# Counting the edges' sources: one-hots of 7 and 6 bits in place of 6 and 7

## The reference, cut to what matters

```
ones = jnp.ones(src.shape[0])
out_deg = jnp.maximum(jax.ops.segment_sum(ones, src, num_segments=n), 1.0)
...
scale = jnp.sqrt(out_deg[src]) * jnp.sqrt(out_deg[dst])
msg = msg / scale[:, None]
```

## Time and profile before

| | us |
|---|---|
| median of 3 runs | 3346.48 (3343.41 to 3349.89) |
| the profiled execution | 3338.86 |
| its span, first to last instruction | 3337.2 |

### The profile page before, as it was taken

How to read it: one execution, slowest core, us unless ns; L and a number is a source line. 1 busy time by engine, 2 the same in 40 slices (tenths; PEclk the granted TensorE clock), 3 DMA queues, 4 the chain that set the end, 5 groups by cost and what they waited for, 6 DMA issues and landing times.

```text
span 3337.2 us, 51572 instructions
## 1 busy us (share of the span) xinstructions
PE 2826.4 (85%) x17241; PEld 2524.3 (76%) x17241; DVE 2173.0 (65%) x5166; ACT 1530.3 (46%) x2926; POOL 1683.0 (50%) x1627
## 2 busy tenths in 40 slices
PE   8858888788888874755799898998989989899998
PEld 8837677678677764744688787887878878788887
DVE  5635555455555565645777878778787877877754
ACT  5102233233233332432456565665656656556565
POOL 0067777777777720245755555454554545543000
PEclk9988899899899986866689999999999999999999
DMA  3176666666666620576777767677676767766534
GB/s 96 49 212 184 189 192 188 189 189 197 191 191 193 195 63 20 183 201 181 231 241 229 228 200 243 198 228 229 212 236 197 234 208 223 237 200 212 158 114 140
DMA packets 369270, 625.86 MB, mean 188 GB/s; under 512 B 86045, under 2 KB 237599, under 8 KB 368995
## 3 DMA queue, kind: packets, MB, share of 16 engines
q1 hardware_dynamic: 290947, 407.51, 38.6%
q0 software_dynamic: 75168, 211.78, 22.5%
q10 hardware_dynamic: 2880, 3.15, 0.3%
HBM read 508.86 MB, written 113.37 MB: 186 GB/s over the span
## 4 chain that ended last, share of the span: by engine, by line
PE 33%; DVE 11%; issue 5%; ACT 3%; POOL 3%; DMA 1%; SPq 0%; DVEq 0%; POOLq 0%; ACTq 0%
PE PB L117 25%; POOL G L2033 3%; PE PB L2089 2%; PE PB L2062 2%; PE PB L2064 2%; DVE WGl L2381 2%; DVE G L2375 2%; DVE XR L2543 2%; PE PB L2077 1%; DVE H1l L2531 1%; ACT TFm L2300 1%; ACT WGh L2227 1%; PE PB L2124 1%; DVE AR L2413 1%; DVE AR L2411 0%
## 5 line engine op out<-in xcount | busy, mean ns | idle before, releaser
L2033 POOL DMA_INDIRECT G<-tab,SRCL x784 | 869.4, 1109 | 801.2 <-DVE WGl L2381 579.4
L862 POOL DMA_INDIRECT G<-tab,SRCL x782 | 772.3, 988 | 264.1 <-issue 241.4
L2300 ACT ACTIVATE TFm<-PB,BIA,SCL 128x512 f32<-128x512 f32 (+1 forms) x416 | 312.6, 751 | 326.8 <-PE PB L117 307.0
L883 PE MATMUL PB<-G,OR 128*128 128x257 f32 x782 | 265.8, 424 | 118.3 <-DMA G<-tab,SRCL 99.2
L117 PE MATMUL PB<-H1h,MW 128*128 128x512 f32 (+1 forms) x832 | 298.8, 403 | 39.6 <-DVE YTMl L2482 26.2
L2227 ACT CAST WGh<-G 128x1056 fp32r<-128x1056 f32 x196 | 210.2, 1072 | 253.2 <-DVE G L2375 252.6
L117 PE MATMUL PB<-MW,H2h 128*128 128x256 f32 x1568 | 298.7, 288 | 11.7 <-DVE H2l L2531 11.6
L117 PE MATMUL PB<-YTMh,MW 128*128 128x512 f32 (+1 forms) x832 | 288.6, 396 | 0.6 <-ACT TF L2265 0.6
L117 PEld LDWEIGHTS PB<-MW,H2h 128*128 128x128 f32 x1568 | 246.4, 192 | 18.1 <-DVE H2l L2531 13.5
L2381 DVE TENSOR_TENSOR WGl<-G,WGh 128x1056 fp32r<-128x1056 f32 x196 | 245.7, 1254 | 21.5 <-ACT WGh L2227 20.6
L2062 PE MATMUL PB<-WGh,OR 128*128 128x264 f32 x784 | 221.7, 309 | 44.5 <-DVE WGl L2381 43.3
(11 more groups left out here) (342 smaller groups left out, 7791.6 us busy)
## 6 DMA issues: line engine op xcount, KB each, us to landing
MW<-msplit SPq DMA_DIRECT2D x312, 512.0 KB
ord<-OR SPq DMA_DIRECT2D x392, 128.0 KB
OR<-ord SPq DMA_DIRECT2D x196, 256.0 KB
ROW<-relrow SPq DMA_DIRECT2D x196, 128.0 KB
G<-tab,SRCL POOLq DMA_INDIRECT x1566
msplit<-FWs SPq DMA_DIRECT2D x68, 256.0 KB, 3.4
tab<-ACC SPq DMA_DIRECT2D x7, 896.0 KB, 7.4
resd<-RSG SPq DMA_DIRECT2D x49, 128.0 KB, 1.9
```

The costliest lines, as they stand in the source:

```text
L862: po.indirect_dma_start(b.G[:, u % RU, q, 0:256], None, c.tab0, bass.IndirectOffsetOnAxis(ap=c.SRCL[:, 2 * u + q:2 * u + q + 1].bitcast(U3 ...
L883: pe.matmul(PB[w % 2][:, 0:257], b.OR[:, u % RH, 0, :], b.G[:, u % RU, 0, :], start=first, stop=False)
L2033: po.indirect_dma_start(b.G[:, j % RP, u, :], None, c.tab1, bass.IndirectOffsetOnAxis(ap=c.SRCL[:, 4 * j + u:4 * j + u + 1].bitcast(U32), ...
L2300: a.activation(b.TM[:, m, 0:n], PB[of][:, 0:n], ACT.Relu, bias=b.BIA[:, l, q:q + 1], scale=b.SCL[:, l, q:q + 1]).then_inc(relu, 1)
```

## The change

The low part gets 7 bits and the high part 6. The weights are now the one-hot of the low part, 128 columns, and the moving operand that of the high part, 49 columns. The region in PSUM is 128 x 49, which is the layout of `DEG` itself, so one instruction takes the maximum. `IOK` grows from 98 to 128 bins; `OH` shrinks from 98 to 49 bins, `OL` grows from 64 to 128. The number of steps, of products and of buffers stays. The sides of the product stay too: the low part is the weights.

```diff
-    b.IOK = sb("IOK", [P, NHI, KB], BF16)
+    b.IOK = sb("IOK", [P, P, KB], BF16)
...
-    b.OL = sb("OL", [P, 2, LO, KB], BF16)
-    b.OH = sb("OH", [P, 2, NHI, KB], BF16)
+    b.OL = sb("OL", [P, 2, P, KB], BF16)
+    b.OH = sb("OH", [P, 2, NT, KB], BF16)
...
-            ins = pe.matmul(PB[0][0:LO, 0:NHI], b.OL[:, i % 2, :, k], b.OH[:, i % 2, :, k], start=(q == 0), stop=(q == 783))
+            ins = pe.matmul(PB[0][:, 0:NT], b.OL[:, i % 2, :, k], b.OH[:, i % 2, :, k], start=(q == 0), stop=(q == 783))
...
-    v.tensor_copy(b.IOK[:, :, :], b.iob[:, 0:NHI].unsqueeze(2).to_broadcast([P, NHI, KB]))
+    v.tensor_copy(b.IOK[:, :, :], b.iob[:, :].unsqueeze(2).to_broadcast([P, P, KB]))
...
-    v.tensor_scalar(b.LOi[:, :], c.SRCL[:, :], LO - 1, None, ALU.bitwise_and)
-    own.done(v.tensor_scalar(b.HIi[:, :], c.SRCL[:, :], 6, None, ALU.logical_shift_right))
+    v.tensor_scalar(b.LOi[:, :], c.SRCL[:, :], P - 1, None, ALU.bitwise_and)
+    own.done(v.tensor_scalar(b.HIi[:, :], c.SRCL[:, :], 7, None, ALU.logical_shift_right))
...
-        v.tensor_tensor(b.OH[:, o, :, :], b.IOK[:, :, :], b.HIb[:, cols].unsqueeze(1).to_broadcast([P, NHI, KB]),
+        v.tensor_tensor(b.OH[:, o, :, :], b.IOK[:, 0:NT, :], b.HIb[:, cols].unsqueeze(1).to_broadcast([P, NT, KB]),
                         ALU.is_equal)
-        v.tensor_tensor(b.OL[:, o, :, :], b.IOK[:, 0:LO, :], b.LOb[:, cols].unsqueeze(1).to_broadcast([P, LO, KB]),
+        v.tensor_tensor(b.OL[:, o, :, :], b.IOK[:, :, :], b.LOb[:, cols].unsqueeze(1).to_broadcast([P, P, KB]),
                         ALU.is_equal).then_inc(S.ol, 1)
...
-    for part in range(2):
-        ins = v.tensor_scalar(b.DEG[LO * part:LO * part + LO, :],
-                              PB[0][0:LO, 0:NHI].rearrange("p (t a) -> p t a", a=2)[:, :, part], 1.0, None, ALU.max)
-    ins.then_inc(S.deg, 1)
+    v.tensor_scalar(b.DEG[:, :], PB[0][:, 0:NT], 1.0, None, ALU.max).then_inc(S.deg, 1)
```

More of the change, by code:

```diff
@@ L31 @@
 NPIECE = 34
-LO = 64
 SPLIT0, SPLITS = 14, 11
 SPLIT_STEPS = {0: "piece", 3: "piece_hi", 5: "piece_lo", 6: "piece_out"}
-NHI = 98
 KSEL = 3124
```

## The result

The changed kernel takes 3293.39 us (median of 4 runs, 3291.01 to 3295.46), the kernel before 3348.18 (4 runs, 3343.41 to 3350.63): 54.8 us less, ratio 0.9838 with a 95% interval from 0.9821 to 0.9855. Forecast were 3297 and a gain of 49. The profiled execution took 3294.54 us with a span of 3292.8.

A forecast was written before the change was run, and what follows sets the result against it. TensorE's histogram pairs were taken to bound `prep`. First load at 8.54, 48 steps x 1.88 = 90.2 and a last step of 2.0 start the degrees at 100.8, 49 us gained in all: 3297 us, range 3283 to 3362.

The forecast's parts named there:

- The bound: Histogram in `prep`: TensorE sets its end, at 149.72 us, and each microsecond there passes to the kernel's end one to one.
- The moving side, 90 to 100 ns: Histogram pair: moving 49 columns for 98, at 1.84 ns a column plus perhaps a fixed cost, takes 90 to 100 ns.
- The weight side, 58 to 235 ns, 108 taken: Histogram pair: loading 128 weight columns for 64, bounded between 58 and 235 ns; 108 chosen from 4-byte loads.
- p: Time of one histogram pair, a weight load overlapped with a matmul: 180 ns before, 108 forecast, 95 to 130 as neighbourhood.
- The far end, 235: Upper end for the 128-column weight load in the histogram: 235 ns, at the moving side's 1.84 ns a column.
- The handshake, 1.88 us a step: Histogram loop: two one-hot buffers hold the step at 1.88 us against TensorE's own 1.73, losing about 0.15 a step.
- The small terms: VectorE builds and start: OL 1.15 us by elements (1.23 in trace), OH 0.47 (0.56), IOK +0.26, first one-hots +0.13.
- (c): Rival, histogram: the strided 128-column load sets the pace; p = 200 gives 3362 us, p = 235 gives 3390; chance 0.21.
- (d): Rival, histogram: the 180 ns pair is a floor of issue or PSUM accumulation, so p stays; 3346 us; chance 0.05.
- (b): Rival, histogram: the load gains only in part, p = 130 to 175; at 150, 23 us gained, 3323; chance 0.11.
- (a): Rival, histogram: load cheaper than moving, p at or below 85 to 95, VectorE and handshake bound; 3284 to 3293; chance 0.13.
- the forecast's own case: Histogram pair p from 95 to 130 ns, 108 taken: 3297 us, own range 3290 to 3308; chance 0.50.

The follow-up runs named there:

- the second run with 28 edge columns: Changed kernel with three one-hot buffers and 28 edge columns a step (28 steps for 49), timed on a second chip: 3282.29 us, 0.9817 of the kernel before.

## Why the prediction was right

- **The bound.** TensorE's pair sets the histogram, the histogram sets `prep`, and its end passes on one to one to the first gather, which moved by 53.9 us with the degrees' 53.97; the median moved by 54.8. For whole times it holds less exactly: in every experiment the time beside the kernel before came out 1 to 14 us better than the shift of the degrees alone (with 127 columns, for instance, the degrees come 45.1 later and the time is 35 longer). Most of these are single runs, and the cause is open.
- **The moving side, 90 to 100 ns.** 98. With 98 columns at 180 and 49 at 98 a column is 82 / 49 = 1.67 ns and 16 ns are fixed (with the 184 ns of 128 x 98 it is 1.76 and 12); I had 1.84 and allowed for a fixed part.
- **The weight side, 58 to 235 ns, 108 taken.** This is the term that was mis-sized, in the good direction. I had the load as the dearer side, which sets p at 108; the load of 128 takes at most 62 ns, so it is hidden, and the moving side sets p. That 108 stands only 10 ns from the measured 98 is luck. The inference "100 ns for 64 columns, so at most 200 for 128" was a misreading: the first two loads start 100 ns apart, but a 64-column load sustains only one in 120 ns. The far end, 235, was the right price for a load of the common kind: 237 with 127 columns. My reason for 108, that loads of 4-byte columns come every 110 ns, bore no relation to what happened. The Trainium skill (TensorE: Matmul & The Clock Gate, Weight-path perf modes) names such a load, a fast one that comes on at exactly 128 weight columns and was measured at about 2x. The runs agree with its condition, 128 against 127, and show more than its 2x: 237 to at most 62 ns. The p of about 100 that I worked out from that rule lay close by luck too, since it took the load for the pace.
- **The handshake, 1.88 us a step.** Right in kind. With p = 98 the same sum gives (0.06 + 1.57 + 0.28 + 1.70) / 2 = 1.80; measured 1.78. It also gives 1.98 for 64 weight columns (measured 1.97) and 1.92 for the kernel before with its moving operand side by side (measured 1.92), but these two hardly test it: TensorE's own 16 x 0.120 = 1.92 is as near. What shows it is the third buffer.
- **The small terms.** OL 1218 ns and OH 564 against 1.23 and 0.56 us; IOK +0.25 us. The first load came 0.29 later where I had 0.13. The sources were awaited until 4.62 us before and 4.79 here, and the first load followed 3.79 and 3.91 later, so 0.12 is the longer one-hots and the rest is when the DMA landed. Two more profiles of the changed kernel have the first load at 8.36 and 8.79 us, both 3.9 behind the sources.
- **Rivals.** (c), slower by 16 to 43 us, has the right mechanism at 127 columns, where its far end is what the change would have cost, 45. (d) is out: pairs came every 42 ns. (b), a pair of 130 to 175 ns, was seen in no kernel here. (a) came nearer than the forecast's own case. Its near end, p = 95 with a step of 1.78 us and 3293 us, is the measured step and time, and its reason, a load cheaper than the moving side, is what the runs show. VectorE's 1.62 now exceeds TensorE's 1.57, as (a) has it; only p itself, 98, falls in the forecast's 95 to 130. With a third buffer VectorE is the bound alone.

The sum again with measured terms: 8.70, 48 x 1.775 = 85.2, and 16 x 0.098 + 0.28 = 1.85, makes 95.75, as measured. As 1.775 is (93.89 - 8.70) / 48 from the same trace, this tests only the tail of 0.28.

## What to carry to other kernels

When a product's operands can trade columns, write the pair as the dearer of two sides, load and moving, each with its own price, and look for a width at which one price jumps: here 127 weight columns cost 237 ns and 128 cost at most 62. A one-hot laid out for VectorE at a step of 32 bytes costs TensorE more than twice the moving time of one side by side (98 ns for 49 columns against at most 42), so give the strided moving side the fewer columns, as long as the load keeps its 128. And when the two engines of a two-buffer loop come near each other, the step is half of their sum with both handovers, so that the third buffer pays only after the change and not before it.

## What the runs showed of the hardware

| weights x moving columns, bf16 | pair, ns |
|---|---|
| 64 x 98, both at 32 bytes | 180 |
| 64 x 98, moving side by side | 120 |
| 64 x 49, both at 32 bytes | 120 to 123 |
| 127 x 49, both at 32 bytes | 237 |
| 128 x 98, both at 32 bytes | 184 |
| 128 x 49, both at 32 bytes | 98 |
| 128 x 49, moving side by side | 62 to 65 |
| 128 x 49, both side by side | 42 |

All at a granted clock of 1.00. Two things I had not expected. A load of the common kind costs 1.87 ns a column at this step at both widths tried, 64 and 127. And at a step of 56 bytes the pair 128 x 49 is a little cheaper than at 32. In the second run with 28 edge columns 55 matmuls, with one start of a step among them, come every (5.37 - 0.27) / 54 = 94 ns on average. Inside a step it is 92 ns, where the changed kernel has 98; why is open.

```profile
36.85 5.37 PE L310 MATMUL PB<-OH,OL 128*128 128x49 bf16 x55
```
